# Stage 0 of a two-layer graph network: the type mask of the edge features moves from VectorE to GpSimd

## The chip, the cores and the metric

The kernel runs on one core of one Trainium2 chip. The metric is the device time of one execution in microseconds, the median of several runs. Before the change three runs took 2187.74, 2188.85 and 2201.08 us.

## The reference, cut to what matters

There are 3125 nodes with 64 features and 100000 edges, sorted by their target node. The first layer (stage 0 of the kernel) computes, for each edge,

```
w5e   = edge_feat @ W5[edge_type] + b5[edge_type]          # 16 features, three edge types
num   = sum(h3[edge_dst] * (h4[edge_src] + w5e))
score = softmax((num / 4)[:, None], axis=-1)[:, 0]
out   = h1 + segment_sum(score[:, None] * (h2[edge_src] + w5e), edge_dst)
x     = layernorm(x + out)
```

The second layer (stage 1) gathers the rows of the new x by edge source, adds a linear map of 32 other edge features, and takes a softmax-weighted sum per channel over the edges of each target node. The change touches stage 0 only.

The weight matrix depends on the edge's type. The kernel does without a choice of weights: it lays the 16 features of an edge three times one above the other (48 rows), sets to zero those copies whose type is not the edge's, and multiplies by the three weight matrices stacked to 48 rows, with three more rows for the biases, whose "feature" is 1. To set those copies to zero is the **mask**: `featm = (types == type_of_row) * feat`.

## The kernel before, in words

**Chunks.** The edges are cut in two halves, and a chunk is 512 edges of each half, so that tiles have 128 partitions: 64 channels of the one half, 64 of the other. There are 98 chunks. Chunk c uses buffers s = c % 2, and r = c // 2 counts how often a pair of buffers has been used.

**Stage 0, one chunk.** SyncE loads the features and types (`load_features0`, four transfers, after `masked` tells that the mask of two chunks before is done), the start rows (`load_inj`) and the keep flags (`load_keep`). GpSimd gathers rows of the table `d_h24` by the edges' source nodes (`gather0`, L605 to L625): one indirect transfer per 128 edges, eight for a chunk, or six for those chunks (71 of 98) of which TensorE makes a quarter itself by products with one-hot matrices. VectorE makes these one-hot matrices (`one_hot0`, L1210, about eight instructions for each chunk), and TensorE multiplies them (`pick0`, L900, three products for each). TensorE then projects the masked features into `q_sum` (`project0`, L909) and adds the gathered rows by transposing them into the same bank (L882, L887); turns the start rows (`turn_inj`, L924), the products (L938), the running sums (L955) and the probabilities (L946). VectorE spreads the target's row over its edges with a scan (`expand`, L1235), multiplies (`products`, L1244), masks (`mask`, L1226), reduces to scores (L1216, L1220), multiplies probabilities and messages (L1258), sums them with a scan (L1263), and makes the probabilities (L1249, L1252). ScalarE copies between banks and buffers (L703 to L742) and stores the result.

**The order** is written out by hand on each engine. In round c VectorE does `expand` and `products` of chunk c, `mask` of chunk c+1, the scores of c-1, the message sums of c-2, the probabilities of c-1, and a piece of one-hot matrices; in its round c TensorE does a piece of `pick0`, `project0` and `turn_inj` of chunk c+1, then the numerator and the second half of the rows of chunk c (L882 and L887 again, which signal `q2_ready`), and the turns of c-2 and c-1. So the round of VectorE is counted here from one `expand` to the next.

**The ring of row buffers.** There are eight buffers for gathered rows (`RING`). GpSimd gathers six chunks ahead of all (`AHEAD`), then scatters the start rows (L646), then gathers chunks 6 and 7, and from chunk 8 on it waits before each chunk's gathers until TensorE has used the buffer of eight chunks before (L620):

```
if c >= RING:
    pool.wait_ge(q2_ready[c % 2], (c - RING) // 2 + 1)
```

Beside these gathers and its two scatters of indices GpSimd does no arithmetic in stage 0.

## Time and profile before

| | |
|---|---|
| runs, us | 2187.74, 2188.85, 2201.08 (median 2188.85) |
| profiled execution: span from first to last instruction, us | 2193.7 (its time is given by this span alone) |
| PE busy | 1808.2 us, 82% |
| DVE (VectorE) busy | 1649.8 us, 75% |
| POOL (GpSimd) busy | 1282.8 us, 58% |
| ACT (ScalarE) busy | 791.6 us, 36% |
| granted TensorE clock, mean | 0.916 |
| stage 0's chunks: first and last expand start, us | 203.1, 1150.7 |

PE is TensorE, PEld its weight loads, SP SyncE. Busy shares are averages over stages; a stage's pace is read from the order of single instructions in time. In a timeline a line shows start, duration, engine, source line, what is written and read, its shape, and in brackets how long the engine was idle before it and what the trace takes for the releaser ("issue": nothing that the profile shows; "remote": an unknown queue). Ends of TensorE's instructions are modelled. The duration of an indirect transfer on POOL is the time in which GpSimd writes its descriptors, not that in which the rows move.

### The profile page before, as it was taken

Reading aid. Unit: us, or ns where it says so; the run is one execution under the profiler, and the core shown is the slowest. Engines: PE = TensorE matmul, PEld = TensorE weight load, DVE = VectorE, ACT = ScalarE, POOL = GpSimd, SP = SyncE. Lnnn points to the kernel's source line nnn. Section 1 sums busy time; section 2 is a strip of 40 time slices with the busy share of each in tenths; the row PEclk is TensorE's granted clock in tenths of the full one; section 3 lists DMA queues with packets and bytes.
Section 4 is the critical chain, followed back from the end, with each engine's and each line's share of the span. In section 5 each row is a group of like instructions: output and inputs, shape, how many; then the busy total and the mean of one; then the engine's idle time right before and its main releaser. Section 6 shows DMA issues by size and latency. Waiting matters only on the chain.

```text
span 2193.7 us, 29535 instructions
## 1 busy us (share of the span) xinstructions
PE 1808.2 (82%) x9200; PEld 1086.3 (50%) x9200; DVE 1649.8 (75%) x3316; ACT 791.6 (36%) x1503; POOL 1282.8 (58%) x1347
## 2 busy tenths in 40 slices
PE   6599999999999999999981678788887878879863
PEld 5334555655555655555560245445444544545432
DVE  6534877878878788788787378778887877878876
ACT  3101223223322333223231145455554545545561
POOL 7365666666666666666614666666666666666624
PEclk9899999999999999999995789889998998989975
DMA  8933445554545555555442245555554545555541
GB/s 283 391 61 94 139 144 148 148 151 144 148 142 153 143 146 145 147 148 152 138 141 58 48 134 156 141 151 157 153 149 142 164 140 162 149 149 153 151 140 57
DMA packets 216065, 321.30 MB, mean 146 GB/s; under 512 B 61931, under 2 KB 123940, under 8 KB 215781
## 3 DMA queue, kind: packets, MB, share of 16 engines
q1 hardware_dynamic: 128950, 148.58, 23.3%
q0 software_dynamic: 43056, 68.05, 13.8%
q10 hardware_dynamic: 43904, 102.79, 13.1%
q8 instruction: 75, 1.23, 0.2%
q14 instruction: 80, 0.66, 0.1%
HBM read 186.00 MB, written 133.22 MB: 146 GB/s over the span
## 4 chain that ended last, share of the span: by engine, by line
PE 29%; issue 26%; DVE 16%; another core or an unknown queue 12%; ACT 11%; ACTq 3%; POOL 1%; DMA 1%; SPq 0%; DVEq 0%; POOLq 0%
PE wide L900 11%; PE wide L999 7%; DVE late L1210 3%; ACT block L819 3%; DVE edge_lists L1210 3%; DVE featm L1226 2%; DVE score L1216 2%; ACTq L812 2%; ACT prob_wide L796 2%; PE wide L1010 2%; ACT msg L797 1%; DVE h3d L1235 1%; ACT block L800 1%; PE wide L860 1%
## 5 line engine op out<-in xcount | busy, mean ns | idle before, releaser
L634 POOL DMA_INDIRECT rows<-d_x,idx x588 | 558.3, 950 | 342.1 <-issue 158.2
L624 POOL DMA_INDIRECT block<-d_h,idx x482 | 455.6, 945 | 278.8 <-issue 126.2
L900 PE MATMUL wide<-late,typed 125*128 125x512 bf16 (+1 forms) x936 | 282.4, 382 | 35.7 <-issue 35.3
L999 PE MATMUL wide<-late,ntype_i 125*128 125x512 bf16 x975 | 239.5, 403 | 53.9 <-DVE ntype_i L1346 49.7
L900 PE MATMUL wide<-edge_lists,typed 125*128 125x512 bf16 (+1 forms) x864 | 259.8, 381 | 22.1 <-issue 20.9
L1235 DVE TENSOR_TENSOR_SCAN h3d<-keep,h3d,bank 128x512 f32<-128x512 bf16 x98 | 125.4, 1280 | 176.4 <-issue 171.2
L999 PE MATMUL wide<-edge_lists,ntype_i 125*128 125x512 bf16 x936 | 223.4, 393 | 11.1 <-issue 11.0
L624 POOL DMA_INDIRECT rows<-d_h,idx x160 | 151.0, 944 | 132.7 <-remote 48.4
L1010 PE MATMUL wide<-ident,block 128*128 128x128 f32 x784 | 135.3, 319 | 93.6 <-ACT block L819 59.3
L999 PEld LDWEIGHTS wide<-late,ntype_i 125*128 125x128 bf16 x975 | 100.9, 104 | 175.9 <-DVE ntype_i L1346 50.1
L900 PE MATMUL wide<-late,ntype_i 125*128 125x512 bf16 (+1 forms) x468 | 179.0, 383 | 3.9 <-issue 3.5
L1210 DVE TENSOR_SCALAR late<-msg,pick_of 125x512 bf16<-125x512 f16 (+1 forms) x468 | 144.6, 375 | 46.1 <-remote 33.9
L722 ACT ACTIVATE q_sb<-wide 128x512 f32<-128x512 f32 x98 | 58.4, 596 | 325.9 <-remote 251.9
L1010 PEld LDWEIGHTS wide<-ident,block 128*128 128x128 f32 x784 | 115.4, 211 | 113.5 <-issue 105.9
L819 ACT ACTIVATE block<-wide 128x512 f32<-128x512 f32 x196 | 106.4, 595 | 179.3 <-remote 154.6
L900 PE MATMUL wide<-edge_lists,ntype_i 125*128 125x512 bf16 (+1 forms) x432 | 164.2, 380 | 5.1 <-issue 5.1
L900 PEld LDWEIGHTS wide<-late,typed 125*128 125x128 bf16 x936 | 90.6, 99 | 146.7 <-issue 54.1
L1210 DVE TENSOR_SCALAR edge_lists<-msg,pick_of 125x512 bf16<-125x512 f16 (+1 forms) x432 | 135.2, 378 | 25.7 <-remote 16.1
L999 PEld LDWEIGHTS wide<-edge_lists,ntype_i 125*128 125x128 bf16 x936 | 94.2, 101 | 121.9 <-issue 28.9
L900 PEld LDWEIGHTS wide<-edge_lists,typed 125*128 125x128 bf16 x864 | 83.4, 99 | 122.3 <-issue 36.2
L1371 DVE SCALAR_TENSOR_TENSOR run<-bank,block 128x512 f32<-128x512 f32 x98 | 67.1, 685 | 84.2 <-ACT block L800 64.6
L1361 DVE TENSOR_TENSOR_SCAN h3d<-bank,h3d,keep 128x511 f32<-128x511 f32 x98 | 125.5, 1281 | 3.5
(224 smaller groups left out, 3390.0 us busy)
## 6 DMA issues: line engine op xcount, KB each, us to landing
d_run<-block ACTq DMA_DIRECT2D x98, 512.0 KB
d_inj<-zeros SPq DMA_DIRECT2D x28, 896.0 KB
inj<-d_inj SPq DMA_DIRECT2D x98, 256.0 KB
d_run<-stage ACTq DMA_DIRECT2D x98, 256.0 KB
feat<-in_ea16x3T SPq DMA_DIRECT2D x196, 96.0 KB
types<-d_type SPq DMA_DIRECT2D x196, 64.0 KB
keep<-d_keep SPq DMA_DIRECT2D x196, 64.0 KB
keep<-d_pen SPq DMA_DIRECT2D x196, 64.0 KB
```

The lines of the kernel that those rows point to most:

```text
L624: pool.indirect_dma_start(out=ring[c % RING][:, j, h, :], out_offset=None, in_=d_h24, in_offset=bass.IndirectOffsetOnAxis(ap=idx[:, c, at: ...
L634: pool.indirect_dma_start(out=rows1[c % RING1][:, j, h, :], out_offset=None, in_=d_x1, in_offset=bass.IndirectOffsetOnAxis(ap=idx[:, c, at ...
L722: act.activation(q2_sb[s][:, :], q_sum[s], ACT.Copy).then_inc(q2_copied[s], 1)
L796: act.activation(up[s], y[s][:, :], ACT.Relu).then_inc(updown_ready[s], 1)
L819: act.activation(stage1[s][:, :, :, q, :], p_out1[:, q * CH:(q + 1) * CH].rearrange("p (j h c) -> p j h c", j=TILES, h=2), ACT.Copy).then_ ...
L900: ins = pe.matmul(p_pick[s][:, 0:cols], table0[n][:, k, :], hot0[b][:, k - b * KT, 0:cols], start=(k == 0 and n == 0), stop=(k == NT - 1 a ...
L999: ins = pe.matmul(p_hot[s], table[q][:, SPLIT * k:SPLIT * (k + 1), :].rearrange("p b c -> p (b c)"), hot[s][:, k, :], start=(k == 0 and q ...
L1010: ins = pe.matmul(p_out1[:, q * CH + j * P:q * CH + (j + 1) * P], src[:, j:CH:TILES], ident[:, :], is_transpose=True, start=True, stop=True)
L1210: ins = dve.tensor_scalar(hot0[b][:, k - b * KT, 0:cols], pick_slots[u % SLOTS][0:NP, 0:cols], pick_of[:, k:k + 1], None, ALU.is_equal)
L1235: dve.tensor_tensor_scan(h3d[s][:, :], keep[s][:, :], p_inj[:, :], h3d[1 - s][:, CH - 1:CH], ALU.mult, ALU.add).then_inc(h3_ready[s], 1)
L1361: dve.tensor_tensor_scan(before[s][:, 1:CH], p_m[c % 3][:, 0:CH - 1], keep[s][:, 1:CH], before[s][:, 0:1], ALU.max, ALU.add).then_inc(befo ...
L1371: dve.scalar_tensor_tensor(mexp[s][:, :], p_m[c % 3][:, :], EPS, expm[s][:, :], ALU.add, ALU.mult).then_inc(mexp_ready[s], 1)
```

## The change

VectorE's `mask` is taken out, at all 98 places in its order. GpSimd gets a `mask(c)` of two instructions: it compares the types with the row's type in place (`tensor_scalar`, bf16), waits for that to be written, and multiplies by the features (`tensor_tensor`, bf16 by f32 to f32), which signals `masked`. Its waits are those of before: the features of the chunk have landed, and `injT` of two chunks before has been signalled, by which TensorE has read the old `featm`. The masks of chunks 0 and 1 come after the scatters of the start rows; from chunk 8 on, ahead of `gather0(c)` with its wait for the row buffer, comes `mask(c - 6)`; the last six masks come after the last gather. One semaphore is added.

```diff
+MASKS_AHEAD = 2
...
+            def mask(c):
+
+                s, r, _ = chunk_of(c)
+                pool.wait_ge(feat_in[s], 16 * 4 * (r + 1))
+                wait(pool, injT[s], r)
+                pool.tensor_scalar(types[s][:, :], types[s][:, :], type_of_row[:, :], None, ALU.is_equal).then_inc(s_own_type, 1)
+                pool.wait_ge(s_own_type, c + 1)
+                pool.tensor_tensor(featm[s][:, :], types[s][:, :], feat[s][:, :], ALU.mult).then_inc(masked[s], 1)
...
+            pool.wait_ge(s_const, 16 * 5)
+            for c in range(MASKS_AHEAD):
+                mask(c)
             for c in range(AHEAD, CHUNKS):
+                if c >= RING:
+                    mask(c - RING + MASKS_AHEAD)
                 gather0(c)
+            for c in range(CHUNKS - RING + MASKS_AHEAD, CHUNKS):
+                mask(c)
...
-            def mask(s, r, c):
-
-                dve.wait_ge(feat_in[s], 16 * 4 * (r + 1))
-                wait(dve, injT[s], r)
-                dve.scalar_tensor_tensor(featm[s][:, :], types[s][:, :], type_of_row[:, :], feat[s][:, :],
-                                         ALU.is_equal, ALU.mult).then_inc(masked[s], 1)
...
-                for work, d in ((expand, 0), (products, 0), (mask, 1), (score_parts, -1), (message_sums, -2), (probabilities, -1)):
+                for work, d in ((expand, 0), (products, 0), (score_parts, -1), (message_sums, -2), (probabilities, -1)):
...
-            for work, back in ((score_parts, 3), (mask, 1), (expand, 2), (products, 2), (probabilities, 3), (message_sums, 4),
+            for work, back in ((score_parts, 3), (expand, 2), (products, 2), (probabilities, 3), (message_sums, 4),
```

## Rows read from the trace of the kernel before

**Rows 1.** Windows view of the rounds paced by gathers: busy us (instructions), clock, DMA share, GB/s.
```profile
229.00:1097.00 868.00, 814.20 (x4525) 503.84 (x4523) 695.22 (x1492) 257.20 (x551) 534.41 (x566) 1.00 0.51 146
```

**Rows 2.** Timeline, GpSimd: start us, us, engine, line, operation, idle before and its releaser.
```profile
609.85 0.94 POOL L624 DMA_INDIRECT rows<-d_h,idx  x1 [2.15 <-remote]
...
616.08 0.94 POOL L624 DMA_INDIRECT rows<-d_h,idx  x1 [0.30 <-issue]
619.21 0.94 POOL L624 DMA_INDIRECT rows<-d_h,idx  x1 [2.18 <-remote]
...
628.19 0.94 POOL L624 DMA_INDIRECT block<-d_h,idx  x1 [1.80 <-PE wide L887]
...
637.38 0.94 POOL L624 DMA_INDIRECT block<-d_h,idx  x1 [2.00 <-PE wide L882]
...
646.10 0.94 POOL L624 DMA_INDIRECT block<-d_h,idx  x1 [0.30 <-issue]
649.62 0.94 POOL L624 DMA_INDIRECT block<-d_h,idx  x1 [2.57 <-remote]
```

**Rows 3.** Timeline, VectorE: each round's first instruction, the scan of `expand`.
```profile
618.71 1.28 DVE L1235 TENSOR_TENSOR_SCAN h3d<-keep,h3d,bank 128x512 f32<-128x512 bf16 x1 [0.79 <-issue]
...
627.91 1.28 DVE L1235 TENSOR_TENSOR_SCAN h3d<-keep,h3d,bank 128x512 f32<-128x512 bf16 x1 [1.15 <-issue]
...
637.10 1.28 DVE L1235 TENSOR_TENSOR_SCAN h3d<-keep,h3d,bank 128x512 f32<-128x512 bf16 x1 [1.09 <-issue]
...
649.34 1.28 DVE L1235 TENSOR_TENSOR_SCAN h3d<-keep,h3d,bank 128x512 f32<-128x512 bf16 x1 [4.15 <-issue]
...
658.45 1.28 DVE L1235 TENSOR_TENSOR_SCAN h3d<-keep,h3d,bank 128x512 f32<-128x512 bf16 x1 [1.02 <-issue]
```

**Rows 4.** Timeline, TensorE, end of one round and start of the next.
```profile
615.59 0.39 PE L887 MATMUL wide<-typed,ident 128*128 128x128 f32 x2
...
617.98 0.60 PE L900 MATMUL wide<-late,typed 125*128 125x512 bf16 x2 [1.06 <-issue]
```

**Rows 5.** Timeline, ScalarE: the copy that waits for TensorE's L887.
```profile
618.97 0.60 ACT L722 ACTIVATE q_sb<-wide 128x512 f32<-128x512 f32 x1 [2.76 <-remote]
```

**Rows 6.** Timeline, ScalarE: a copy late in stage 0, after the last gather.
```profile
1123.76 0.60 ACT L742 ACTIVATE stage<-bank 128x512 f32<-128x512 f32 x1 [0.27 <-PE bank L946]
```

**Rows 7.** Waits, GpSimd, 400 to 1000 us: us in total, times, longest.
```profile
POOL block L624 <- remote: 65.8, 31, 2.6
POOL rows L624 <- remote: 30.3, 14, 2.5
POOL block L624 <- PE wide L882: 21.8, 10, 3.0
...
POOL block L624 <- PE wide L887: 13.2, 6, 2.7
```

**Rows 8.** Groups by line, VectorE, 400 to 1000 us: busy us, mean ns, idle before.
```profile
L1226 DVE SCALAR_TENSOR_TENSOR featm<-types,type_of_row,feat 128x512 f32<-128x512 bf16 x61 | 45.4, 745 | 0.0
```

**Rows 9.** Timeline, VectorE: one round's one-hot matrices.
```profile
615.18 2.75 DVE L1210 TENSOR_SCALAR late<-msg,pick_of 125x512 bf16<-125x512 f16 x9
```

**Rows 10.** Timeline, VectorE, last rounds of stage 0.
```profile
1111.12 0.74 DVE L1226 SCALAR_TENSOR_TENSOR featm<-types,type_of_row,feat 128x512 f32<-128x512 bf16 x1
1111.78 0.68 DVE L1216 TENSOR_REDUCE score<-bank 128x8 f32<-128x512 f32 x1
...
1136.88 0.74 DVE L1226 SCALAR_TENSOR_TENSOR featm<-types,type_of_row,feat 128x512 f32<-128x512 bf16 x1
...
1142.42 0.75 DVE L1226 SCALAR_TENSOR_TENSOR featm<-types,type_of_row,feat 128x512 f32<-128x512 bf16 x1 [0.72 <-DMA feat<-in_ea16x3T]
```

**Rows 11.** Groups by line, GpSimd: its fill of a 128x512 tile.
```profile
L594 POOL MEMSET feat<- 128x512 f32 x2 | 1.0, 519 | 0.0
```

**Rows 12.** Timeline, GpSimd, before and after the gathers of chunks 6 and 7.
```profile
179.34 0.98 POOL L624 DMA_INDIRECT block<-d_h,idx  x1 [3.08 <-remote]
...
211.75 0.94 POOL L624 DMA_INDIRECT rows<-d_h,idx  x1 [14.72 <-PE wide L887]
```

More of the change, by code:

```diff
@@ L308, in gnn_program @@
         mexp_ready, s_run, n_run, max_out = sems("mexp_ready"), sems("s_run"), sems("n_run"), sems("max_out")
-        s_ones1 = sem("s_ones1")
+        s_ones1, s_own_type = sem("s_ones1"), sem("s_own_type")
         feat1_in = feat_in + inj_in
```

## The prediction

> **What bounds the kernel now.** I read the page's totals first, and they mislead: TensorE 82% busy, VectorE 75%, GpSimd 58%. From 229 to 1097 us, the part of stage 0 in which GpSimd gathers, TensorE is busy for 814 of 868 us [rows 1]. So I read the timeline for the length of single rounds, from one `expand` to the next. They come in two lengths: 618.71 to 627.91, to 637.10, to 649.34, to 658.45, which is 9.20, 9.19, 12.24 and 9.11 us [rows 3]. In GpSimd's timeline the long round is the one with eight gathers; the others have six [rows 2]. The difference, 3.0 us, is two gathers at 1.25 us from start to start and half a microsecond. Neither VectorE's nor TensorE's work in a round depends on whether its GpSimd issues six gathers or eight, so it is GpSimd that sets the length.
>
> How it does so: GpSimd starts a set 0.3 us after `expand` (619.21 to 618.71, 649.62 to 649.34), issues six gathers in 7.18 us (from 609.85 to 616.08 plus 0.94), and then stands idle for 2.18, 1.80 or 2.00 us, after eight gathers for 2.57 us [rows 2]. What it waits for is TensorE's use of an old buffer (L887, `q2_ready`). TensorE's L887 is recorded as done at 615.98 [rows 4], yet ScalarE's copy, which waits for the same signal, starts only at 618.97 [rows 5], and GpSimd at 619.21: the signal reaches its readers 1.6 to 2.3 us after the last gather of the set has been issued. Where no gather runs, a turn of TensorE's is answered within 0.27 us [rows 6]. I cannot say what holds the signal; the time at which it comes goes with the gathers. The pattern is general: between 400 and 1000 us there are 61 such waits, one for each chunk, 131.1 us in all, 2.15 us on the average [rows 7].
>
> So the loop is: gathers (7.18 us for six), then about 2.0 us until the signal, then gathers again. The idle 2.0 us (2.57 after eight) is the space into which the change puts the mask.
>
> **What the change removes.** 98 masks of 745 ns on VectorE [rows 8]; a round loses 0.66 us, the time from the mask's start to that of the next instruction (1111.12 to 1111.78) [rows 10]. In the gathers' rounds VectorE is idle for 0.79 to 4.15 us ahead of `expand` [rows 3], so this is off the path and worth nothing there; what covers it is GpSimd's set with its signal. After the last gather VectorE has five masks, at 1111.12 to 1136.88, without an idle time ahead of them, and one that waits 0.72 us for its features [rows 10]. Five times 0.66, plus 0.66 and perhaps a part of the 0.72, gives 4 us; bounds 0 (another wait takes it) and 5.
>
> **What it adds: the price of a mask on GpSimd.** The trace shows no two-operand instruction there. Nearest is a fill of a 128x512 tile, 519 ns [rows 11]; the other neighbour is VectorE's fused mask, 745 ns. The compare reads one tile and writes one: between 0.52 and 1.04 (twice the fill); I take 0.75, the time that VectorE needs for both steps. The product reads two: between 0.52 and 1.49 (twice VectorE's), and I take 1.2, somewhat over two fills, one for each operand. There are three gaps: before the compare, for the wait between the two, and before the next gather; gathers follow each other with 0.30 [rows 2], and I take 0.2 each (bounds 0.1 and 0.3). Sum 0.75 + 1.2 + 0.6 = 2.55 us, between 1.34 and 3.43.
>
> The Trainium skill (GPSIMD Engine Reference, 3.1) gives 2.6 cycles an element for a two-input operation there, from which I estimate 1.1 us for the product, and measured 769 ns for a tight loop over 512 elements. No row here shows either; by them the mask would be 1.87 + 0.6 = 2.5 us, and the sum nearly the same.
>
> **What of it lies on the path.** After six gathers 2.0 us are free, so 0.55 us sticks out, and the next set starts that much later. After eight 2.57 are free and nothing sticks out. Of 98 chunks eight are gathered ahead; of the 90 sets behind, 23 have eight gathers and 67 six. About five of these, at the start of stage 0, are not yet paced by GpSimd. So 62 x 0.55 = 34 us. Bounds: at 1.34 us nothing; at 3.43 us 62 x 1.43 + 23 x 0.86 = 108.
>
> **What is moved.** The mask issues no transfer. It passes one queue, GpSimd's. Behind it stand its wait for the row buffer and the gathers; those are wanted seven rounds later, so only the length of the loop counts. The mask of chunk c+2 now comes at the end of round c, while TensorE wants it in round c+1 after its piece of `pick0`, some 5 us after `expand`; VectorE's came in c+1 as well. New waits: for the features of c+2, issued a round earlier, and for `injT` of chunk c, signalled with this round's `expand`. Both are there when six gathers have been issued: no wait. SyncE's feature loads wait for `masked`, which comes earlier than before: nothing. At the start, masks 0 and 1 (5.1 us) go behind the scatters, where GpSimd is idle for 3.08 us; the 2 us that stick out delay the gathers of chunks 6 and 7, after which it is idle for 14.72 us [rows 12]: nothing. One-hot matrices end 0.66 us sooner, but their user TensorE is held by the same signal.
>
> **Sum.** 2193.7 + 34 - 4 = 2224 us for the profiled span, which is 4.9 us above the median of the runs. So I predict 2219 us, 1.4% slower. About 1%, 22 us, is what a measurement of this kernel tells from no change.
>
> **Rivals.**
> - *The mask fits into the idle time* (up to 2.0 us): the four microseconds at the end remain, 2185 us. For it: two operations at the fill's price and small gaps are 1.34 us. Against: a fill reads nothing. 0.20.
> - *The signal waits for GpSimd as a whole, not for the gathers.* If what holds it ends about 1.6 us after whatever GpSimd did last, the whole mask adds to each of 90 rounds: 90 x 2.55 - 4 = +226, 2415 us; at the low price, 2305. For it: I don't know the cause of the hold, and the trace has nothing but gathers there. Against: after eight gathers it lasts 2.3 us, not 1.6, which fits rows still landing better than an engine at rest. 0.12.
> - *VectorE's chain sets the six-gather rounds after all*, and ends on the faster side. Its one-hot matrices end at 617.93 [rows 9], TensorE starts their products at 617.98 after 1.06 us idle [rows 4], and `expand` follows at 618.71. If the signal came with that start, a shorter chain would bring it 0.66 us sooner as long as GpSimd is ready: 62 x 0.66 = 41, and 4, 2144 us. It decides only where the mask on GpSimd takes less than 1.3 us, or gathers get along without the signal. Against: the round with eight gathers is 3 us longer with the same work on VectorE. 0.18.
> - *The two engines collide.* VectorE's one-hot stretch of 2.75 us [rows 9] would overlap GpSimd's mask. It ran from 615.18 to 617.93 and will end near 617.3, while the mask starts at 617.1: some 0.3 us more in 62 rounds, 19 us, 2238 us. 0.05. The Trainium skill (SBUF — State Buffer, "two separate sides") speaks against the change here: in its two-port modes VectorE takes a port pair that GpSimd's operations need, as an exclusive lock. By that rule the sum would be this rival's. No row here shows GpSimd reading a tile, so whether the trace agrees is open.
>
> **How the numbers follow.** The forecast has 0.45, with 2190 (a mask of 2.1 us) to 2290 (nearly the upper bound, 2293) as its own range. The range 2145 to 2290 takes in the mask that fits, the collision and half of the faster case; the other half (0.09) and the whole mask in each round (0.12) lie outside, 0.2 together. Faster by over 1% (below 2167): 0.18. Within 1%: 0.20 and the cheap end of the forecast, 0.09, so 0.29. Slower: 0.53.
>
> **What would show it.** Right: two GpSimd operations per chunk that take about 1.95 us together; the idle time ahead of a set's first gather is nearly gone after six; rounds of 9.7 us with six gathers and still 12.2 with eight; VectorE idle about 2 us ahead of `expand`; rounds after 1109 us shorter by 0.7. Wrong at the price: operations of 0.5 or of 1.5 us each. Wrong at the mechanism: rounds longer by the whole mask, also those with eight gathers; or six-gather rounds below 9.1 us. Wrong at the cover: the compare waiting for features or for `injT`, or TensorE idle ahead of L909.

## The result: 4.4% slower, three times what was forecast

| | before | after |
|---|---|---|
| time, us, median of three (lowest to highest) | 2188.85 (2187.74 to 2201.08) | 2285.51 (2284.82 to 2294.47) |
| ratio, 95% interval | | 1.0439 (1.0393 to 1.0485) |
| span of the profiled execution, us | 2193.7 | 2283.0 |
| `expand` of chunk 0, of 91, of 97 starts at, us | 203.1, 1109.2, 1150.7 | 203.3, 1196.6, 1243.9 |
| mean round, `expand` of 8 to 90, us | 9.97 | 11.07 |
| rounds with six, with eight gathers, us | 9.23, 12.14 | 10.16, 13.73 |

The medians differ by 96.7 us, the two spans by 89.3. Of these, 87.4 come up to the expansion of chunk 91, 5.8 in the six rounds behind it, and 3.9 are given back by the rest of the kernel. So the loss is in the rounds with gathers, where the forecast put it, but it is 1.10 us per round instead of 0.55, and the rounds with eight gathers pay too.

GpSimd's timeline over two rounds, the answer to [rows 2]:

```profile
610.31 1.04 POOL L634 DMA_INDIRECT block<-d_h,idx  x1 [0.15 <-issue]
...
616.71 0.95 POOL L634 DMA_INDIRECT block<-d_h,idx  x1 [0.30 <-issue]
617.70 1.82 POOL L611 TENSOR_SCALAR types<-types,type_of_row 128x512 bf16<-128x512 bf16 x1
619.60 1.16 POOL L613 TENSOR_TENSOR featm<-types,feat 128x512 f32<-128x512 bf16 x1
620.91 1.05 POOL L634 DMA_INDIRECT block<-d_h,idx  x1 [0.15 <-issue]
```

From the end of the last gather (617.66) to the next set there are 3.25 us instead of the 2.18 of [rows 2], and no wait is left in them: 1.82 of comparison, 1.16 of product, 0.27 of gaps. From chunk 15 to 97 this slot is 3.09 us in the mean, against 2.15 us of idle time before, and a set of six gathers lasts 7.34 us instead of 7.18. The groups by line give the prices over all 98 chunks (busy us, mean ns, idle before):

```profile
L634 POOL DMA_INDIRECT block<-d_h,idx x482 | 465.3, 965 | 144.5 <-issue 134.0 <-remote 8.4
L611 POOL TENSOR_SCALAR types<-types,type_of_row 128x512 bf16<-128x512 bf16 x98 | 161.6, 1649 | 25.2 <-DMA feat<-in_ea16x3T 18.9 <-PE bank L941 3.0
...
L613 POOL TENSOR_TENSOR featm<-types,feat 128x512 f32<-128x512 bf16 x98 | 113.8, 1161 | 8.2
```

The waits of [rows 7] are gone; beside the 0.3 us between gathers GpSimd is not idle from 300 to 1100 us. The granted clock from 200 to 1000 us is 0.96 instead of 1.00, but TensorE has time to spare there: the wait has moved to TensorE, as the list of waits from 200 to 1200 us (us in total, times, longest) and TensorE's timeline show:

```profile
PEld wide L926 <- POOL featm L613: 155.7, 67, 4.3
PE wide L926 <- POOL featm L613: 122.7, 65, 3.8
```

```profile
610.21 1.13 PE L926 MATMUL wide<-featm,w 128*128 128x512 f32 x2 [3.53 <-POOL featm L613]
...
620.81 1.12 PE L926 MATMUL wide<-featm,w 128*128 128x512 f32 x2 [1.31 <-POOL featm L613]
```

VectorE's timeline, the answer to [rows 3, 9]:

```profile
612.43 1.28 DVE L1245 TENSOR_TENSOR_SCAN h3d<-keep,h3d,bank 128x512 f32<-128x512 bf16 x1 [4.00 <-PE bank L941]
...
617.71 4.05 DVE L1227 TENSOR_SCALAR late<-msg,pick_of 125x512 bf16<-125x512 f16 x8
622.93 1.28 DVE L1245 TENSOR_TENSOR_SCAN h3d<-keep,h3d,bank 128x512 f32<-128x512 bf16 x1 [1.17 <-issue]
```

Eight one-hot matrices took 4.05 us beside GpSimd's comparison, nine took 2.75 before. The comparison itself takes 1.58 us at its shortest hereabouts (at 607.33, where VectorE has little to do) and 1.82 here. The two engines do slow each other. What GpSimd loses by it lies in its slot and so in the round; the one-hot matrices do not end the round, since TensorE waits for the mask.

### The profile page after: what moved, and what is told of

Same layout as the page of the kernel before. It is cut to its first block, busy times and chain, and to the rows that moved or that the text cites. A ratio compares the mean times of both kernels' runs of the same rounds, so it can differ in the third digit from the quotient of the medians.

```text
span 2283.0 us, 29634 instructions
## 1 busy us (share of the span) xinstructions
PE 1830.6 (80%) x9200; PEld 1105.5 (48%) x9200; DVE 1672.2 (73%) x3218; ACT 799.7 (35%) x1503; POOL 1575.3 (69%) x1543
## 4 chain that ended last, share of the span: by engine, by line
POOL 37%; issue 16%; PE 16%; ACT 11%; another core or an unknown queue 11%; DVE 4%; ACTq 3%; DMA 1%; SPq 0%; POOLq 0%; DVEq 0%
POOL block L634 18%; POOL types L611 7%; POOL rows L634 6%; PE wide L1016 5%; PE wide L917 5%; POOL featm L613 5%; ACT block L836 3%; ACTq L829 2%; ACT prob_wide L813 2%; ACT msg L814 2%; ACT block L817 1%; ACT block L806 1%; PE wide L1027 1%; PE wide L877 1%
## 5 line engine op out<-in xcount | busy, mean ns | idle before, releaser
L634 POOL DMA_INDIRECT block<-d_h,idx x482 | 465.3, 965 | 144.5 <-issue 134.0
L917 PE MATMUL wide<-late,typed 125*128 125x512 bf16 (+1 forms) x936 | 277.8, 379 | 14.7 <-issue 14.5
L1016 PE MATMUL wide<-late,ntype_i 125*128 125x512 bf16 x975 | 231.1, 393 | 53.3 <-DVE ntype_i L1356 49.9
L1016 PE MATMUL wide<-edge_lists,ntype_i 125*128 125x512 bf16 x936 | 236.9, 410 | 10.7 <-issue 10.4
L926 PE MATMUL wide<-featm,w 128*128 128x512 f32 x196 | 115.8, 674 | 129.6 <-POOL featm L613 129.5
L1227 DVE TENSOR_SCALAR late<-msg,pick_of 125x512 bf16<-125x512 f16 (+1 forms) x468 | 179.4, 450 | 50.2 <-remote 38.6
L1227 DVE TENSOR_SCALAR edge_lists<-msg,pick_of 125x512 bf16<-125x512 f16 (+1 forms) x432 | 169.9, 459 | 20.1 <-remote 11.5
L611 POOL TENSOR_SCALAR types<-types,type_of_row 128x512 bf16<-128x512 bf16 x98 | 161.6, 1649 | 25.2 <-DMA feat<-in_ea16x3T 18.9
```

Of the source, the lines that this page charges most:

```text
L611: pool.tensor_scalar(types[s][:, :], types[s][:, :], type_of_row[:, :], None, ALU.is_equal).then_inc(s_own_type, 1)
L634: pool.indirect_dma_start(out=ring[c % RING][:, j, h, :], out_offset=None, in_=d_h24, in_offset=bass.IndirectOffsetOnAxis(ap=idx[:, c, at: ...
L917: ins = pe.matmul(p_pick[s][:, 0:cols], table0[n][:, k, :], hot0[b][:, k - b * KT, 0:cols], start=(k == 0 and n == 0), stop=(k == NT - 1 a ...
L926: pe.matmul(q_sum[s], w5[:, :], featm[s][:, :], start=True, stop=True)
L1016: ins = pe.matmul(p_hot[s], table[q][:, SPLIT * k:SPLIT * (k + 1), :].rearrange("p b c -> p (b c)"), hot[s][:, k, :], start=(k == 0 and q ...
L1227: ins = dve.tensor_scalar(hot0[b][:, k - b * KT, 0:cols], pick_slots[u % SLOTS][0:NP, 0:cols], pick_of[:, k:k + 1], None, ALU.is_equal)
```

## The experiments

Theory A: a round lasts as long as GpSimd's gathers (about 7.3 us for six, 9.8 for eight, 7.95 in the mean) and the larger of two things behind them: the 2.15 us until the row buffer's signal, or the work put into that slot. Against it stand B (the work adds whole), C (other engines' waits cost, not GpSimd's time) and D (VectorE's chain sets the rounds). "The slot" is the place between two sets of gathers. Each kernel was timed beside the kernel before on its own chip, so the ratios compare, the times between chips don't.

**GpSimd work of known size in the slot: `fills2`, `fills4`, `fills6`.** The kernel before, with n memsets (n = 2, 4, 6):

```diff
             for c in range(AHEAD, CHUNKS):
+                if c >= RING:
+                    for _ in range(n):
+                        pool.memset(spare[:, :], 0.0).then_inc(s_spare, 1)
+                        fills += 1
+                        pool.wait_ge(s_spare, fills)
                 gather0(c)
```

> The kernel before (VectorE masks), with two GpSimd memsets of a spare 128x512 tile, one after the other, in the slot ahead of the wait for a row buffer of each chunk from 8 on: about 2 x 0.60 us of extra GpSimd time and nothing else. Theory A (GpSimd's loop decides, and its idle of 2.0 to 2.2 us per chunk takes up the first 2.0 us of any work put into that slot): no change, 2185 to 2195 us, rounds still 9.97 us in the mean. Rival B (the row buffer's signal moves out by whatever GpSimd does, so that work in the slot adds whole): 90 x 1.2 = +108, about 2297 us. Rival C (GpSimd's time is not what lengthens the changed kernel; it is the wait of TensorE for the mask, or VectorE slowed by GpSimd): no change, as A.

> The same with four memsets, about 2.4 us in the slot. Theory A: the excess over 2.15 us, 90 x 0.25 = +23, about 2212 us (2195 to 2230); rounds about 10.2 us. Rival B: +216, about 2405 us. Rival C: no change, 2185 to 2195.

> The same with six memsets, about 3.6 us in the slot. Theory A: 90 x (3.6 - 2.15) = +130, about 2319 us (2300 to 2335), and GpSimd's waits for the row buffer gone; the changed kernel's 3.25 us lies between this one and that with four, and its +97 should lie on the line between them (by A 90 x (3.25 - 2.15) = +99). Rival B: +324, about 2513 us. Rival C: well under +97, since the changed kernel has other costs beside GpSimd's time: under 2285 us.

Ratios 1.0184 (1.0161 to 1.0206), 1.0025 (1.0011 to 1.0039), 1.0498 (1.0478 to 1.0517). Six memsets fill the slot like this, and with four and six there is no wait for a buffer from 300 to 1100 us:

```profile
704.71 3.59 POOL L654 MEMSET spare<- 128x512 f32 x6
708.57 0.95 POOL L626 DMA_INDIRECT block<-d_h,idx  x1 [0.27 <-POOL spare L654]
```

From the set of chunk 15 to that of 97, GpSimd's mean cycle was 10.59 us with four and 11.80 with six. This is its own work: 7.98 us of gathers and a slot of 2.61 with four, 7.99 and 3.81 with six. With the mask it is 7.99 + 3.09 = 11.09. So GpSimd's time sets the pace of the changed kernel's rounds; C falls, and B too (six would have cost 324 us and cost 112).

The cost of the kernel as a whole did not go as A said. A had 2212 us and rounds of 10.2 us for four memsets, 23 us more than before, and they cost 7 us with rounds of 9.91 (chunks 8 to 90). Nor does the changed kernel lie on the line between four and six. From the first expansion to the last they took 960.5 and 1067.1 us, which makes 1003 us for a slot of 3.09; the changed kernel took 1040.6. What lies between, 37 us, is the part behind the last gather, as the next paragraphs show.

Two memsets, 1.2 us in a slot of 2.15, cost 1.8%: the signal came later (2.47 us behind the set in the mean instead of 2.15) and single gathers lasted 1.4 us instead of 0.94.

```profile
607.84 0.95 POOL L626 DMA_INDIRECT block<-d_h,idx  x1 [0.31 <-issue]
609.09 0.95 POOL L626 DMA_INDIRECT block<-d_h,idx  x1 [0.30 <-issue]
610.04 1.12 POOL L654 MEMSET spare<- 128x512 f32 x2
612.35 0.95 POOL L626 DMA_INDIRECT block<-d_h,idx  x1 [1.19 <-remote]
613.60 1.46 POOL L626 DMA_INDIRECT block<-d_h,idx  x1 [0.30 <-issue]
```

Four memsets cost almost nothing in the end, although GpSimd's last gather came 56 us later (1163.2 us; 1107.1 before). In the kernel before, the chain runs 60 us behind the gathers and has 43.6 us of work left after the last one. With four memsets it ran 9.45 us a round from chunk 14 to 34, came up to 6 us behind, and was 2.5 us behind the last gather (with six, 1.9 us). So the lead, the time from the end of a chunk's gathers to its expansion, paid for most of the memsets. The changed kernel's last gather is late too (1204.2 us), but it has 39.7 us left behind it; its lead stays at 63 us to the end. That led to `spread`, below.

**No mask at all: `nomask`.** VectorE's mask is left out and TensorE multiplies the unmasked features, so the result is another one. TensorE then waits for the features themselves, and SyncE's next load for `injT` instead of `masked`.

```diff
-                for work, d in ((expand, 0), (products, 0), (mask, 1), (score_parts, -1), ...
+                for work, d in ((expand, 0), (products, 0), (score_parts, -1), ...
...
-                pe.matmul(q_sum[s], w5[:, :], featm[s][:, :], start=True, stop=True)
+                pe.matmul(q_sum[s], w5[:, :], feat[s][:, :], start=True, stop=True)
```

> The kernel before without any mask: the queries' product takes the edge features unmasked, and no engine compares or multiplies; everything else stands. Theory A (GpSimd's gathers and the signal that follows them set each round, VectorE's 745 ns lie beside): rounds unchanged at 9.97 us; only behind the last gather do VectorE's 5 or 6 masks come off the chain: 2184 us (2180 to 2190). Rival D (VectorE's chain sets the six-gather rounds, so taking 745 ns off it shortens them): 61 x 0.75 = -46, about 2143 us.

Ratio 0.9943 (0.9922 to 0.9963), the rounds 9.95 us in the mean, the last six 36.0 us instead of 41.5. D falls: VectorE's 745 ns were off the path. So a mask that costs no engine anything would have brought some 0.6%.

**The price by itself: `price`.** Behind the end of the kernel before, GpSimd runs each form five times in a chain, for example

```diff
+            pool.wait_ge(s_x1, 2 * GROUPS)
+            for _ in range(5):
+                pool.tensor_scalar(b, b, row, None, ALU.is_equal).then_inc(s_bench, 1)
+                n += 1
+                pool.wait_ge(s_bench, n)
```

> The kernel before, and behind its end, with every other engine done, GpSimd operations on 128x512 tiles five times each in a chain: the comparison as in the change (bf16 from bf16 with a scalar from a 128x1 tile), the same with a constant, a multiplication in its place, the comparison into f32 and from f32, a constant multiplication f32, copies bf16 and f32, the product from bf16 and f32, the product from f32 and f32; then comparison and product again while VectorE runs bf16 comparisons of 128x512 one after another. Theory N (the comparison's 1.6 us is its own price, whatever runs beside it): 1.56 to 1.60 us here too. Theory O (it comes from the scalar that is read from a tile): 0.8 to 1.0 us with a constant. Theory Q (it comes from the 2-byte type): about 0.8 to 1.0 us from f32 into f32. Theory R (VectorE's small operations beside it in the kernel stretch it): under 1.2 us here, 1.6 beside VectorE. The product 1.15 us in all. Of the 0.24 us between its shortest and longest in the changed kernel, all by VectorE beside it: 1.58 alone, 1.83 or more with it.

Groups by line. L685 is the comparison alone, L693 a multiplication by the same scalar, L701 the comparison in f32, L705 a multiplication in f32 by a constant, L717 the product, L713 a copy; L725 and L729 are comparison and product beside VectorE's comparisons:

```profile
L725 POOL TENSOR_SCALAR types<-types,type_of_row 128x512 bf16<-128x512 bf16 x5 | 8.4, 1680 | 0.5
L685 POOL TENSOR_SCALAR types<-types,type_of_row 128x512 bf16<-128x512 bf16 x5 | 7.8, 1563 | 12.5 <-DVE typed L1341 12.2
L693 POOL TENSOR_SCALAR types<-types,type_of_row 128x512 bf16<-128x512 bf16 x5 | 7.8, 1563 | 0.5
...
L701 POOL TENSOR_SCALAR spare<-spare,type_of_row 128x512 f32<-128x512 f32 x5 | 7.8, 1560 | 0.5
L705 POOL TENSOR_SCALAR spare<-spare 128x512 f32<-128x512 f32 x5 | 7.4, 1488 | 0.4
...
L729 POOL TENSOR_TENSOR spare<-types,spare 128x512 f32<-128x512 bf16 x5 | 5.8, 1158 | 0.4
L717 POOL TENSOR_TENSOR spare<-types,spare 128x512 f32<-128x512 bf16 x5 | 5.8, 1158 | 0.4
...
L713 POOL COPY spare<-spare 128x512 f32<-128x512 f32 x5 | 3.1, 613 | 0.3
```

Theory N holds, in one run: the comparison costs 1.56 us alone, as a multiplication or in f32 as well, 0.08 less with a constant. It is the kind of operation, one tile and a scalar, that costs 2.5 copies and a third more than the product of two tiles.

**One half of the mask on each engine: `prod_dve`, `cmp_dve`, `cmp_dve2`.** In `prod_dve` GpSimd compares and VectorE multiplies:

```diff
                 pool.tensor_scalar(types[s][:, :], types[s][:, :], type_of_row[:, :], None, ALU.is_equal).then_inc(s_own_type, 1)
-                pool.wait_ge(s_own_type, c + 1)
-                pool.tensor_tensor(featm[s][:, :], types[s][:, :], feat[s][:, :], ALU.mult).then_inc(masked[s], 1)
...
+                dve.wait_ge(s_own_type, c + 1)
+                dve.tensor_tensor(featm[s][:, :], types[s][:, :], feat[s][:, :], ALU.mult).then_inc(masked[s], 1)
```

> The changed kernel with the product back on VectorE (ahead of its score sums) and only the comparison (1.6 us, with its start 1.75) in GpSimd's slot. GpSimd waits for nothing of VectorE's there. Theory A (round = the larger of what the rest allows, 9.97 us with the signals' lag or 9.05 without, and GpSimd's 7.95 + 1.75 = 9.7): ratio 1.00 to 1.005 on a chip with the lag, 1.025 to 1.03 without. Theory A2 (with the lag, work in the slot costs though it is shorter than the idle, as two memsets of 1.2 us did with 0.57 us a chunk): 10.5 to 10.8 us per round, ratio 1.018 to 1.035 with the lag. Rival B (adds whole): +1.75 per chunk, ratio 1.065 with the lag.

Ratio 1.0045 (1.0024 to 1.0065), rounds 10.04 us. This is A's clearest case: 1.58 us of work in the changed kernel's own slot, and the buffer's signal is still what the gathers wait for.

```profile
613.49 1.58 POOL L611 TENSOR_SCALAR types<-types,type_of_row 128x512 bf16<-128x512 bf16 x1
615.76 1.11 POOL L632 DMA_INDIRECT rows<-d_h,idx  x1 [0.68 <-remote]
```

In `cmp_dve` it is the other way round, VectorE compares and GpSimd multiplies:

```diff
-                pool.tensor_scalar(types[s][:, :], types[s][:, :], type_of_row[:, :], None, ALU.is_equal).then_inc(s_own_type, 1)
                 pool.wait_ge(s_own_type, c + 1)
                 pool.tensor_tensor(featm[s][:, :], types[s][:, :], feat[s][:, :], ALU.mult).then_inc(masked[s], 1)
...
+                dve.tensor_scalar(types[s][:, :], types[s][:, :], type_of_row[:, :], None, ALU.is_equal).then_inc(s_own_type, 1)
```

> The changed kernel with the comparison alone back on VectorE (in place, bf16, before its score sums), the product alone left on GpSimd in the same slot: GpSimd's slot holds 1.16 us and a start of about 0.1. Theory A (GpSimd's cycle per chunk is the gathers' 7.3 us and the larger of the slot's work and the 2.15 us of idle before the row buffer's signal): the slot's work fits, rounds 9.97 to 10.1 us, 2190 to 2200 us (ratio 1.00 to 1.005). Theory A2 (as A, but the run with two memsets showed that even 1.2 us in the slot costs 0.57 us per chunk, since the signal comes 0.3 us later and single gathers stretch from 0.95 to 1.4 us): about 10.5 us per round, 2235 us (ratio 1.018). Rival B (work adds whole): +1.3 per chunk, 2300 us.

> The kernel with the comparison on VectorE and only the product (1.16 us) in GpSimd's slot, again, beside the kernel before on the same chip. On a chip without the lag: GpSimd's 7.95 + 1.34 = 9.29 us against TensorE's 9.05, ratio 1.015 as measured. On a chip with the lag: theory A says the slot's 1.34 us lie within the 2.15 us of idle, rounds 9.97 to 10.1, ratio 1.00 to 1.005; theory A2 (a lagging signal comes later when the slot holds work, as with two memsets) 10.5 us, ratio 1.018.

The first ran at 1.0146 (1.0130 to 1.0161) on a chip of another kind (below), the second at 1.068 (1.0652 to 1.0709), slower than the whole mask. No theory had that. GpSimd's timeline of the second:

```profile
610.93 0.94 POOL L631 DMA_INDIRECT rows<-d_h,idx  x1 [0.31 <-issue]
615.77 1.16 POOL L610 TENSOR_TENSOR featm<-types,feat 128x512 f32<-128x512 bf16 x1 [3.90 <-DVE types L1240]
617.08 0.98 POOL L631 DMA_INDIRECT block<-d_h,idx  x1
```

GpSimd waits for VectorE's comparison (615.34), which stands behind VectorE's `expand` (613.42), which waits for a signal of TensorE's that comes 1.55 us after the last gather. The product then stands behind the signal instead of beside it: 5.2 us between these two sets, 3.7 in the mean. I had costed the work and not the wait that I added.

**The order of masks and gathers: `spread`, `spread2`, and the tail: `tail_dve`.** `spread` does the same work, with the masks drawn nearer to the gathers, one chunk at every eighteenth:

```diff
+            masks = MASKS_AHEAD
             for c in range(AHEAD, CHUNKS):
-                if c >= RING:
-                    mask(c - RING + MASKS_AHEAD)
+                while c >= RING and masks <= c - RING + MASKS_AHEAD + (c - RING) // 18:
+                    mask(masks)
+                    masks += 1
                 gather0(c)
```

> The changed kernel with GpSimd's masks moved nearer to the gathers by one chunk at every eighteenth: mask of chunk c-6 stands ahead of the gathers of chunk c at first, as in the changed kernel, mask of chunk c-2 at the end, so that two masks instead of six stand behind the last gather. The same work on every engine. Theory E (GpSimd is the bound in every round, and the mask of chunk c-6 right ahead of the gathers of chunk c holds the chain 6 chunks behind the gathers, so that six chunks are left when they end): the last gather ends about 4 x 3.1 = 12 us later (1217), but the last expansion comes at about 1226 instead of 1244 us: 18 us off the changed kernel, ratio to the kernel before about 1.035 (2267 us by the changed kernel's 2285). Rival F (the tail is TensorE's and VectorE's own chain, whatever GpSimd's order): the last expansion stays 40 us behind the last gather or moves out: 1244 to 1256, ratio 1.044 to 1.05.

> The spread order again (mask of chunk c-6 ahead of the gathers of c at first, of c-2 at the end, the same work in all), beside a tail on VectorE on the same chip. On the chip without the lag the last gather came at 1201.9 us and the last expansion 16.1 us behind it. Theory E (GpSimd bounds the rounds, the order keeps the chain six chunks behind): last gather 12 us later than in the changed kernel, last expansion 16 us behind it instead of 40: 12 us off the changed kernel, ratio 1.035 with the lag (changed kernel 1.040 to 1.044), 1.086 without (the changed kernel then 1.092). Rival F (order without effect): 1.040 to 1.044, or 1.09.

`spread2` ran at 1.0365 (1.0338 to 1.0393); the changed kernel again, `after2`, at 1.0403 (1.0381 to 1.0425). The intervals overlap, the traces decide. From the first expansion to the last the changed kernel took 1040.6 us, `after2` 1040.8, `tail_dve` (below, on the chip of `spread2`) 1042.6, `spread2` 1027.9, and its last expansion came 17.1 us behind the last gather. Theory E holds, 13 us for an expected 12: with mask c-6 ahead of gathers c, TensorE can't come nearer than six chunks to the gathers, so the kernel pays for GpSimd's load and, unlike the one with memsets, for an undiminished run-out too. The whole run-out can't be had back by the order: six masks of 3.1 us would have to come ahead of the last gather, 19 of the 37 us (an estimate). `spread` itself ran where the changed kernel was not timed (1.0863, 1.0846 to 1.0880; last expansion 16.1 us behind the last gather).

`tail_dve` gives the masks of the last six chunks back to VectorE (whose part is left out here).

```diff
             def mask(c):
                 s, r, _ = chunk_of(c)
+                if c < 0 or c >= 92:
+                    return
```

> The changed kernel with the masks of chunks 92 to 97, those behind GpSimd's last gather, back on VectorE; the others stay on GpSimd. Theory A: rounds with gathers unchanged (11.05 us in the mean), the tail from the expansion of chunk 91 to that of 97 takes 41.5 us as before instead of 47.3: 6 us off, ratio 1.0375 with the lag, 1.089 without. Rival T (the tail is longer for another reason, such as the wait for features): 47 us still, ratio 1.040 to 1.044, or 1.092.

Ratio 1.0407 (1.0380 to 1.0435), last six rounds 46.5 us, 1042.6 us from first to last expansion: no gain, rival T. The first of these rounds fell from 14.68 to 10.96 us; the other five grew from 32.6 to 35.5. Both have late features in them, of which the changed kernel's GpSimd shows most:

```profile
1213.02 1.17 POOL L613 TENSOR_TENSOR featm<-types,feat 128x512 f32<-128x512 bf16 x1
1222.50 1.56 POOL L611 TENSOR_SCALAR types<-types,type_of_row 128x512 bf16<-128x512 bf16 x1 [8.31 <-DMA feat<-in_ea16x3T]
```

**A possible better version: `tail_pool`, `tail_pool2`.** VectorE masks chunks 0 to 91 as before, and GpSimd the last six, when it is idle. Both run the same kernel.

```diff
             def mask(c):
                 s, r, _ = chunk_of(c)
+                if c < 92 or c >= 98:
+                    return
```

> VectorE masks chunks 0 to 91 as in the kernel before, GpSimd masks chunks 92 to 97 alone, behind its last gather, where it has nothing else to do. Theory A: rounds with gathers as before; of the tail, 41.5 us in the kernel before and 36.0 without any mask, 4 to 5.5 us come off: 2184 us, ratio 0.998 (0.997 to 0.999). Rival I (GpSimd's mask of 3.0 us sets the tail's rounds, as in the changed kernel, whose tail is 47.2 us): 2192 us, ratio 1.002.

> VectorE masks chunks 0 to 91, GpSimd the last six, again. On the chip without the lag the ratio was 1.0017. With the lag, theory A: rounds unchanged, the tail from the expansion of chunk 91 to that of 97 from 41.5 us to 36 to 38: ratio 0.997 to 0.999. Rival V (in the changed kernel the first round behind the last gathers took 3.7 us longer with the masks on GpSimd than on VectorE, and the later ones 3 us less, so that nothing is left): 0.999 to 1.002.

1.0017 (1.0008 to 1.0026) and 0.9995 (0.9980 to 1.0010). The rounds of chunks 93 and 94 are 0.6 us shorter each, but that of 95 is 10.4 us long instead of 8.1, and the last six take 41.7 us. Nothing is gained, and no kernel here that does the whole computation beats the one before.

**Every second chunk: `half`.** GpSimd masks the even chunks, VectorE the odd ones.

```diff
             def mask(c):
                 s, r, _ = chunk_of(c)
+                if c % 2:
+                    return
```

> The changed kernel with the masks of odd chunks back on VectorE, those of even chunks on GpSimd in their slots, so 3.1 us in every second slot. Theory A, slot by slot (each slot's excess over the 2.15 us of idle adds): 0.95 us in every second round, +0.5 per chunk, about +42 us, ratio 1.019 with the signals' lag. Theory U (GpSimd's mean load decides, 7.95 + 1.55 = 9.5 us against 9.97, and the ring evens it out): 1.000 to 1.005 with the lag. Without the lag the mean load is over TensorE's 9.05 by either: 1.02 to 1.05.

Ratio 1.0218 (1.0188 to 1.0248). GpSimd's mean load, 9.5 us, was below the 9.97 that the rest allows, and yet it cost 2%: theory A, slot by slot. The ring does not even it out.

**One gather fewer: `five`.** The kernel before, with the last of the six gathers left out (old rows stay in the buffer, so the result is another one) in 61 chunks. `gathers_of` is the number of gathers with that one left out.

```diff
-                    for j in range(tiles_of(c)):
+                    for j in range(tiles_of(c) - (h == 1 and gathers_of(c) % 2)):
```

> The kernel before with the last of the six gathers left out in each six-gather chunk from 16 on (that part of the rows keeps older contents), 1.25 us less on GpSimd in 61 chunks. With the lag, theory A (gathers, then the lagging signal, set the round): six-gather rounds 9.23 - 1.25 = 7.98 us if nothing else is near. Rival S (TensorE's own work, 9.02 us per chunk in every round on the chip without the lag, is right behind): 9.0 us, so 0.2 us off a round, 12 us in all. Without the lag: rounds stay 9.02 by both, since TensorE is busy throughout.

A single run took 2143.0 us against a median of 2193.7. The six-gather rounds fell by 1.06 us to 8.17, near A's 7.98, but those with eight rose from 12.14 to 12.84, with 2.8 us of idle instead of 2.1. The mean is 9.37, and TensorE is busy for 781.78 of 800 us:

```profile
200.00:1000.00 800.00, 781.78 (x4414) 491.11 (x4413) 664.70 (x1450) 248.58 (x527) 468.50 (x489) 1.00 0.52 149
```

So both are right in part: gathers and their signal set the single round, and TensorE is next, 0.6 to 0.9 us per round below.

**Paced: `paced`.** `fills4`, with memsets on chunks 8 to 49 only.

```diff
-                if c >= RING:
+                if RING <= c < 50:
                     for _ in range(4):
```

> The kernel before with four GpSimd memsets ahead of the row buffer's wait on chunks 8 to 49 only, none from 50 on. With four memsets throughout, the chain ran 9.45 us per chunk while it caught up from 60 to 6 us behind the gathers, against 9.97 in the kernel before. Theory G (the chain runs at TensorE's own pace of about 9.45 us per chunk whenever GpSimd does not wait on it in step): it does so to the end of the catching up, and on while GpSimd, now without memsets, builds its lead again: last expansion 20 to 40 us earlier than in the kernel before, ratio 0.98 to 0.99. Rival H (a quiet stretch behind each block of gathers is what lets TensorE's signals out; without memsets and without a wait there is none, and the chain goes slower until the ring is full): rounds from 50 on are 9.97 us or longer until the ring is full and then 9.97: ratio 0.995 to 1.01.

Ratio 1.0076 (1.0061 to 1.0092). It says nothing on G or H, because it ran on a chip where the kernel before already goes at TensorE's pace.

**The same kernels on another chip: `before2`, `after2`.**

> The kernel before, unchanged, for a trace on the same chip as the three runs beside it: the chip of the four runs with a comparison on VectorE, a spread order, pacing and a tail on GpSimd ran it in 1917 us, the chip of the runs with memsets in 2208. Theory K (the two kinds of chip differ in when TensorE's signals become visible: 2.3 us after they are sent in the median on the one, 0.01 us on the other): whichever chip this is, the time goes with that lag: about 2190 to 2210 us with a median lag over 2 us and GpSimd idle 2.15 us per chunk, or about 1917 us with none and TensorE busy in all of 200 to 1000 us. Rival L (the difference is one of the clock or of DMA, and the lag is only how the trace records it): a time near the one with a lag of the other.

> The changed kernel, unchanged. Theory A (round = the larger of what the rest allows, and of GpSimd's gathers, 7.95 us per chunk in the mean, plus the slot's 3.1 us): rounds of 11.05 us on any chip. On a chip whose signals lag: ratio 1.044 again. On one without the lag the rest allows 9.05 us, so 83 x 2.0 = +166 and the tail's 6: about 2090 us against 1917, ratio 1.09. Rival M (the change costs the same time everywhere, about 97 us): ratio 1.05 there.

`before2` 2208.9 us with rounds of 10.02 and a median lag of TensorE's signals of 2.27 us; `after2` 1.0403, with 11.08. Theory K holds as far as this chip goes; what the change costs where there is no lag was not measured on the changed kernel itself.

## Why the prediction was wrong, step by step

- **What bounds the kernel before:** right for the single round. `nomask` and `five` show it: VectorE's mask is worth nothing in these rounds, a gather is worth 1.06 us. But TensorE is close behind (9.37 us a round in `five`). Two readings were off: `expand` leads the set by 0.50 us at 618.71, not 0.3, and the idle time after eight gathers is 2.36 us in the mean, not the 2.57 of the one place read.
- **The price of the mask: the step that failed.** Forecast 2.55 us (0.75 comparison, 1.2 product, 0.6 gaps), upper bound 3.43; measured 3.0 to 3.25, 3.09 in the mean, of it 1.65 comparison in the mean, 1.16 product, 0.27 gaps. The product was right within 4%. The comparison was taken at VectorE's price for both steps, with twice a memset as its upper bound; it costs three memsets and lies outside its own bounds. A memset reads nothing and says little about an operation with a scalar. The Trainium skill (GPSIMD Engine Reference, 3.1) gives the 769 ns as the best case, of a tight loop over 512 elements, and does not speak of this form, which took twice that; its 2.6 cycles an element for the two-input product, estimated at 1.1 us, agree with 1.158. So the estimate by the page, 2.5 us, was as low as the forecast.
- **What of it lies on the path:** right in kind, wrong in number. The 2.0 us of idle did absorb that much (`prod_dve`), and in this order of masks the excess added one for one. But with 3.1 us the sets of eight gathers, costed at nothing, stick out too: GpSimd's cycle, from the end of one set to the end of the next, grew from 11.83 to 12.96 us with eight and from 9.34 to 10.41 with six. The sum 62 x 0.55 = 34 becomes, for all 82 rounds from 8 to 89, 82 x 1.10 = 90. Of this the slot makes 78, with the measured idle times: 62 x (3.10 - 2.08) behind sets of six and 21 x (3.06 - 2.36) behind sets of eight. The other 12 are gathers that themselves last 0.15 us longer a set, a term that the prediction did not have. The time came out inside the stated range, 2145 to 2290, near its end; the range was wide enough, the comparison's own bound was not.
- **The tail, -4:** wrong in sign. It became 5.8 us longer. Of the last six rounds the later five did get 1.8 us shorter together, but the first, 7.18 us before, takes 14.68: it still has a set of gathers beside it and three masks behind that on GpSimd, the third waiting for features. I had counted VectorE's masks away and not asked what GpSimd's cost there.
- **The wait for features and for `injT`:** right while gathers run. The start, at nothing: right (203.3 against 203.1).
- **The rivals.** The mask that fits is what `prod_dve` makes of it, 0.45% and not 0. "The whole mask adds" is refuted by `fills6`. VectorE's chain is refuted by `nomask`. The collision was seen: the comparison went from 1.56 to 1.68 us beside VectorE in `price` and to 1.82 in the kernel, one-hot matrices from 0.38 to 0.45 us in the mean. VectorE pays more than GpSimd: its comparison in `price` takes 0.35 us alone and 1.20 beside the product, whose 1.158 us stay as they are. The Trainium skill (SBUF — State Buffer, "two separate sides") has the shared ports as a lock for a whole instruction. The trace agrees beside the product, not beside the comparison, in whose 1.68 us two of VectorE's end. The collision's part of the loss is what it adds to GpSimd's slot, 0.09 us of 3.1 in the mean (1.65 against 1.56), and perhaps a part of the longer gathers.
- **Not foreseen:** that the order ties TensorE to a place six chunks behind the gathers; by `spread2` about 13 us of the loss could be had back by the order alone. The prediction had the mask ready before TensorE wants it, and named TensorE idle ahead of L909 as a sign of being wrong. It is idle there (L926 now, up to 3.8 us). This wait costs nothing in GpSimd's loop, but it is the tie that keeps the run-out long.

What stays open: why two memsets of 1.2 us cost 1.8% and a comparison of 1.6 us in the same slot 0.45%. The longer gathers are not the difference. In both runs they are those that start while VectorE makes `featm` from two tiles (1.27 us in the mean in `fills2`, 1.37 in `prod_dve`, about 0.95 otherwise), and a set of gathers lasts 8.10 us in the one and 8.21 in the other. The difference is the time from a set to the next, 2.47 and 1.86 us, and why the signal comes later beside the memsets is not shown.

## What to carry to other kernels

Idle time of an engine in front of a wait is a budget with an edge: work up to it can be nearly free (`prod_dve`, though not `fills2`), and each microsecond beyond it lengthens that engine's every round, however idle it looks on the average. Whether the kernel pays it depends on the lead that the engine has: four memsets used up a lead of 60 us and cost 7, the masks in their fixed order could not. So the price of the moved operation must come from the same kind of operation on the same engine; where the trace has none, take the bounds wide enough that a factor of three over a fill is inside. And ask of every moved step what it now stands in front of: a wait added there (`cmp_dve2`) or a fixed place in the order (`spread2`) can cost more than the work.

## What the runs showed of the hardware

**TensorE's signals can lag, and not on every chip.** The trace records when an instruction ended (modelled for TensorE) and when the signal it sends changed its semaphore; the time between is called the lag here. In the kernel before, TensorE's signals from 300 to 1000 us lag 2.29 us in the median and 6.0 at most; in `before2`, `nomask`, `price`, `half` and `tail_pool2`, on three chips, 2.2 to 2.7; in the kernels whose GpSimd never waits less (0.35 in the changed kernel, 0.6 in `fills4`), and in `five` 0.5. In the run-out of the kernel before, without gathers, it is 0.01, and VectorE's and ScalarE's signals show 0.01 in the median throughout. On the chip of `cmp_dve`, `spread`, `paced` and `tail_pool` TensorE's took 0.01 us in spite of the same gathers. There ScalarE's copy starts 0.04 us after the end of TensorE's L904 (here from `tail_pool`), while [rows 4, 5] have 2.99 us between them:

```profile
611.71 0.39 PE L904 MATMUL wide<-typed,ident 128*128 128x128 f32 x2
```

```profile
612.14 0.60 ACT L739 ACTIVATE q_sb<-wide 128x512 f32<-128x512 f32 x1 [3.29 <-PE wide L904]
```

That chip ran the kernel before in 1917 us, the others in 2189 to 2212. `tail_pool` had rounds of 9.08 us there and TensorE busy in all of 200 to 1000 us, and 865 us from its last expansion to the end, where the kernel before has 1043:

```profile
200.00:1000.00 800.00, 800.00 (x4576) 509.97 (x4574) 709.97 (x1516) 264.68 (x556) 550.91 (x575) 1.00 0.56 161
```

The clock was 1.00 in that stretch on both. Behind the last expansion it was 0.92 in `tail_pool` and 0.84 in the kernel before, so the 178 us there can't be put down to the lag alone. What makes the difference between the chips the runs do not show. It is the same idle time that the change wanted to use: on the chip without the lag even the product alone (1.17 us) cost 1.5%, and all masks in the spread order 8.6%.
